# Loading the next batch's x in four pieces, and projecting inside the third group of heads

## What is computed

```python
q = split_heads(x @ Wq.T + bq)              # x: (8, 1024, 512)
k = split_heads(x @ Wk.T + bk)
v = split_heads(x @ Wv.T + bv)
q_lr = jnp.einsum('bhtd,hdr->bhtr', q, Wq_lsr)
k_lr = jnp.einsum('bhtd,hdr->bhtr', k, Wk_lsr)
scores = jnp.einsum('bhir,bhjr->bhij', q_lr, k_lr) * scale
scores = jnp.where(causal_mask, jnp.float32(-jnp.inf), scores)
y = jnp.einsum('bhij,bhjd->bhid', _softmax(scores), v)
x = _layernorm(x + y.transpose(0, 2, 1, 3).reshape(Bq, Tq, D_MODEL) @ Wo.T + bo)
```

## Time and profile before

| | us |
|---|---|
| median of 3 runs | 3893.7 (3890.47 to 3897.09) |
| the profiled execution, in all | 3893.05 |
| its span on the core | 3891.3 |
| TensorE busy | 3630.7 (93%) |
| VectorE busy | 2260.8 (58%) |
| ScalarE busy | 1488.4 (38%) |
| GpSimd busy | 666.7 (17%) |

### The profile page before, as it was taken

One profiled execution on the slowest core, in us unless ns is written; L12 is line 12 of the kernel. 1 busy time (PEld: TensorE's weight loads), 2 busy tenths in 40 slices (PEclk: granted clock), 3 DMA queues, 4 the chain that ended last, 5 costly groups with the idle time before them and its releaser, 6 DMA issues. The chain is left out here.

```text
span 3891.3 us, 55460 instructions
## 1 busy us (share of the span) xinstructions
PE 3630.7 (93%) x19935; PEld 2505.5 (64%) x19935; DVE 2260.8 (58%) x4972; ACT 1488.4 (38%) x2793; POOL 666.7 (17%) x859
## 2 busy tenths in 40 slices
PE   4899999999999999999999737999999999999995
PEld 3555556556555555565555337888888888888884
DVE  2576665675765766657657475444444444544456
ACT  1253443443444434434434322333333333333335
POOL 2022121121121221211211201011111111111113
PEclk8999999999999999999999855999999999999997
DMA  5234234233323252332332203343343343444448
GB/s 169 61 93 127 76 92 123 62 97 112 102 72 113 79 142 64 101 110 71 89 115 66 72 0 99 100 139 117 112 131 111 120 124 111 130 121 117 143 157 308
DMA packets 207200, 423.14 MB, mean 109 GB/s; under 512 B 45840, under 2 KB 48912, under 8 KB 198800
## 3 DMA queue, kind: packets, MB, share of 16 engines
q1 hardware_dynamic: 180304, 367.47, 30.6%
q0 software_dynamic: 14400, 35.14, 4.6%
q10 hardware_dynamic: 12288, 17.83, 1.7%
HBM read 246.23 MB, written 72.38 MB: 82 GB/s over the span
## 5 line engine op out<-in xcount | busy, mean ns | idle before, releaser
L833 ACT ACTIVATE probs<-scores_t 128x512 f32<-128x512 f32 (+3 forms) x1536 | 656.8, 496 | 574.6 <-PE scores_t L700 516.9
L1801 PE MATMUL m_ps_h<-m_tokens_t,m_w_parts 128*128 128x512 f32 x3072 | 739.7, 391 | 1.6 <-DVE m_tokens_t L1683 1.6
L1801 PE MATMUL m_ps_y<-m_w_parts,m_hidden_parts 128*128 128x512 f32 x3072 | 737.3, 390 | 0.6
L1801 PEld LDWEIGHTS m_ps_y<-m_w_parts,m_hidden_parts 128*128 128x128 f32 x3072 | 575.3, 188 | 125.8 <-issue 6.3
L1801 PEld LDWEIGHTS m_ps_h<-m_tokens_t,m_w_parts 128*128 128x128 f32 x3072 | 575.3, 188 | 120.1 <-issue 2.0
L889 DVE CUSTOM_DVE_ANT_0 shared_banks<-shared_banks,mask_q_rows 128x128 f32<-128x128 f32 (+3 forms) x1024 | 477.7, 515 | 176.4 <-PE shared_banks L657 173.9
L657 PE MATMUL shared_banks<-k_operands,q_operands 96*128 96x512 f32 (+3 forms) x1536 | 509.3, 379 | 23.7 <-DVE natural L880 8.9
L700 PE MATMUL scores_t<-q_operands,k_operands 128*128 128x512 f32 (+3 forms) x1536 | 494.7, 372 | 33.3 <-ACT probs L833 26.1
L1619 ACT ACTIVATE m_hidden<-m_ps_h,m_b 128x512 f32<-128x512 f32 x256 | 176.6, 690 | 791.1 <-PE m_ps_h L1801 777.9
L562 POOL TENSOR_SCALAR_AFFINE_SELECT probs<-probs 128x256 f32<-128x256 f32 x512 | 220.3, 433 | 1341.3 <-ACT probs L833 1340.7
L657 PEld LDWEIGHTS shared_banks<-k_operands,q_operands 96*128 96x128 f32 x1536 | 279.0, 191 | 263.7 <-issue 122.9
(11 more groups left out here) (243 smaller groups left out, 3225.2 us busy)
## 6 DMA issues: line engine op xcount, KB each, us to landing
m_w_raw<-in_w1T SPq DMA_DIRECT2D x64, 1024.0 KB, 5.2
m_w_raw<-in_w2T SPq DMA_DIRECT2D x64, 1024.0 KB, 7.5
wqk_group<-scratch_wqk SPq DMA_DIRECT2D x32, 1024.0 KB, 5.6
q_operands<-natural SPq DMA_DIRECT2D x192, 128.0 KB, 2.6
k_operands<-natural SPq DMA_DIRECT2D x192, 128.0 KB, 2.7
q_operands<-natural SPq DMA_DIRECT2D x384, 64.0 KB, 2.0
k_operands<-natural SPq DMA_DIRECT2D x384, 64.0 KB, 2.0
natural<-in_xT SPq DMA_DIRECT2D x8, 2048.0 KB, 9.8
```

Source lines behind the costliest of these rows:

```text
L833: act.activation(probs[:, slot_of(k, h // 2), h % 2, c0:HALF], st[:, (HG * k + h) % SCORE_BANKS, c0:HALF], ACT.Exp, scale=SCALE).then_inc( ...
L1801: mm = pe.matmul(bank, a, b, start=(first and n == 0), stop=(final and n == len(pairs) - 1))
```

## The change

1. The next batch's x is loaded in four DMAs of 32 partitions (512 KB each). The piece of head h - 1 is issued behind the strips of head h in slot 1's end, and waits only for the strips of head h - 1; the last piece waits for head 3's. The weights that were issued ahead of x now follow it. The first x of the program is also four DMAs.
2. Slot 2 projects its lower halves at positions 38 and 43 instead of 46 and 47, and copies the lower strips inside the slot (`HALVED` = 3); at its end only upper strips remain.
3. ScalarE's copies of x move from (7, 0), (7, 2), (8, 0), (8, 2) to (5, 2), (6, 0), (6, 2), (7, 0); GpSimd's subtraction from weigh 6 to weigh 3; VectorE's from (8, 3) to (7, 1).
4. Slot 3 uses the same table and order of maxima, and the same inversions, as the slots before it. It had a table of its own, by whole heads, whose first maximum came at position 9.

```diff
-HALVED = 2
+HALVED = 3
-MAX_EARLY = (1, 1, 0, 2, 0, 2, 2, 1, 0, 0, 2, 1, 0, 0, 0, 3, 0, 0, 1, 1,
...
-MAX_LATE = (0, 0, 0, 0, 0, 0, 0, 0, 0, 2, 2, 1, 1, 0, 3, 0, 0, 0, 3, 0,
...
-MAX_AFTER = (MAX_EARLY,) * 3 + (MAX_LATE,)
-PROJ_AFTER = ((27, 42, 56, 57),) * HALVED + ((46, 47, 56, 57),) * 2
+MAX_AFTER = (1, 1, 0, 2, 0, 2, 2, 1, 0, 0, 2, 1, 0, 0, 0, 3, 0, 0, 1, 1,
...
+PROJ_AFTER = ((27, 42, 56, 57),) * 2 + ((38, 43, 56, 57), (46, 47, 56, 57))
-X_HI_AT = ((7, 0), (7, 2), (8, 0), (8, 2))
+X_HI_AT = ((5, 2), (6, 0), (6, 2), (7, 0))
-X_LO_AT = 6
-X_LO_DVE_AT = (8, 3)
-INVERT_AFTER = ((((30, 36, 42, 45), (2, 6, 10, 14)),) * 3 + (((30, 42, 45, 45), (0, 4, 4, 5)),))
+X_LO_AT = 3
+X_LO_DVE_AT = (7, 1)
+INVERT_AFTER = ((30, 36, 42, 45), (2, 6, 10, 14))
...
-            def load_x(b, n):
-
-                for h in range(HG):
-                    sp.wait_ge(strips_sent[h], n * STRIPS)
-                for half in lower_sent:
-                    sp.wait_ge(half, n // GROUPS * HALVED * LOWER_STRIPS)
-                sp.dma_start(nat[:], xT_dram.rearrange("(c p) t -> p c t", p=P)[:, :, bass.ds(b * T, T)]
+            def load_x(b, h):
+
+                rows = slice(DH * h, DH * h + DH)
+                sp.wait_ge(strips_sent[h], b * GROUPS * STRIPS)
+                sp.wait_ge(lower_sent[h // 2], (b * HALVED - 1) * LOWER_STRIPS)
+                sp.dma_start(nat[rows], xT_dram.rearrange("(c p) t -> p c t", p=P)[rows, :, bass.ds(b * T, T)]
                              ).then_inc(x_in, 16)
...
+                    if x_of is not None and h > 0:
+                        load_x(x_of, h - 1)
+                if x_of is not None:
+                    load_x(x_of, HG - 1)
...
+                lower_strips(b, 0)
+                strips(b, 0, first=HALF, weights=GROUPS - 1)
+                lower_strips(b, 1)
+                strips(b, 1, first=HALF, x_of=b + 1 if more else None)
                 if more:
-                    load_x(b + 1, b * GROUPS + GROUPS)
-                    strips(b, GROUPS - 2)
+                    load_w(0)
+                    lower_strips(b, 2)
+                    strips(b, 2, first=HALF)
                     load_w(1)
...
-                                act.wait_ge(x_in, 16 * (b + 2))
+                                act.wait_ge(x_in, 16 * HG * (b + 2))
```

More of the change, by code:

```diff
@@ L237, in plan_slot @@
         order += [("proj", g, i) for i, at in enumerate(PROJ_AFTER[g]) if at == n]
[L238 removed]
+        order += [("invert", g, 0, i) for i, at in enumerate(INVERT_AFTER[0]) if at == n]
         if g > 0:
[L240 to L242 removed]
+            order += [("invert", g - 1, 1, i) for i, at in enumerate(INVERT_AFTER[1]) if at == n]
+        order += [("max", g, i) for i in range(done, done + MAX_AFTER[n])]
+        done += MAX_AFTER[n]
         if n == JOIN_AFTER:
@@ L356, in build_attention @@
         LOWER_STRIPS = STRIPS * HG // 2
-        steps, maxes = attend_steps(), [max_steps(g) for g in range(GROUPS)]
+        steps, halves_first, by_head = attend_steps(), max_steps(False), max_steps(True)
         NE = len(steps)
@@ L455, in lower_strips, with strips @@
                                          ).then_inc(lower_sent[h // 2], 16)
-            def strips(b, slot, lead=False, heads=range(HG), first=0, weights=None):
+            def strips(b, slot, lead=False, heads=range(HG), first=0, weights=None, x_of=None):
                 g = (slot + AHEAD) % GROUPS
@@ L474, in strips @@
                                      ).then_inc(strips_sent[h], 16)
+                    if x_of is not None and h > 0:
+                        load_x(x_of, h - 1)
+                if x_of is not None:
+                    load_x(x_of, HG - 1)
             def run(b):
                 more = not (b == NB - 1)
-                for slot in range(HALVED):
-                    lower_strips(b, slot)
-                    early = slot + 1 < HALVED
-                    strips(b, slot, first=HALF, weights=(slot + AHEAD + 1) % GROUPS if early else None)
-                    if more and not early:
-                        load_w((slot + AHEAD + 1) % GROUPS)
+                lower_strips(b, 0)
+                strips(b, 0, first=HALF, weights=GROUPS - 1)
+                lower_strips(b, 1)
+                strips(b, 1, first=HALF, x_of=b + 1 if more else None)
                 if more:
-                    load_x(b + 1, b * GROUPS + GROUPS)
-                    strips(b, GROUPS - 2)
+                    load_w(0)
+                    lower_strips(b, 2)
+                    strips(b, 2, first=HALF)
                     load_w(1)
@@ L511, in store @@
                 sp.dma_start(table[bass.ds(b * T + t * P, P), 0:D], xn[:, t % 2]).then_inc(xn_out[t % 2], 16)
-            load_x(0, 0)
+            for h in range(HG):
+                rows = slice(DH * h, DH * h + DH)
+                sp.dma_start(nat[rows], xT_dram.rearrange("(c p) t -> p c t", p=P)[rows, :, 0:T]).then_inc(x_in, 16)
             load_w(0)
@@ L884, in run @@
                     elif kind == "max":
-                        h, slot, it, k0, n = maxes[item[1]][item[2]]
+                        h, slot, it, k0, n = (by_head if lead else halves_first)[item[2]]
                         dve.wait_ge(bank_full[bank], off[bank] + turn + 1)
```

10 lines of the change are left out of this document (4 added, 6 removed).

## The result

| | before | after |
|---|---|---|
| median, us | 3893.7 | 3953.6 (3952.2 to 3955.4) |
| ratio, 95% interval | 1 | 1.0154 (1.0136 to 1.0172) |
| span of the profiled execution, us | 3891.3 | 3953.7 |
| slot 2, sum over seven batches | 392.2 | 461.1 |
| slot 3, batch 3 | 52.1 | 50.2 |

The change makes the kernel slower by 60 us, 1.5%. The forecast was 3930 us with a range from 3895 to 3962; sign and range held, and the loss was 1.6 times the one forecast.

What follows compares the result with a forecast made beforehand. TensorE, busy 93% of the span, was taken as the bound, losing time in slot 2 to late x and lower clock. Slot 2 +49.2, slot 3 -14 and start +1.5 gave +36.7 us: 3930 us, range 3895 to 3962.

Steps and rivals of the forecast that it cites:

- Term A: Slot 2: ScalarE asks for x before it lands, so TensorE waits 5.0 us before a score of step 6.
- lower clock behind A: Slot 2: after the gap at step 6's score TensorE runs at its lower clock, losing 2.9 us.
- Term B: Slot 2: VectorE's moved subtractions precede a maximum that frees a bank, so TensorE waits 2.85 us near step 7.
- lower clock behind B: Slot 2: TensorE's second gap, waiting for VectorE, brings a second stretch of lower clock, losing 2.0 us.
- banks behind the projections: Slot 2: the second maximum behind the projection waits 0.3 us for the bank VectorE frees after the projection's copy.
- The rival on slow pieces: Load of x: 32-row pieces take 6.2 us to land, making TensorE's gap 6.9 us; 3944 us, chance 0.18.
- Term C: Slot 3: its maxima can begin at once, giving slot 0's length: 2.1 us less per batch, 14 us in seven.
- The start: Program start: first x in four pieces means three more issues ahead of its landing, taken as 1.5 us more.
- rival 1: Slot 2: x's pieces land in time, so the wait for x and its clock loss vanish; 3875 us, chance 0.09.
- rival 2: Slot 2: VectorE's subtractions are covered, only the place of the wait moves; no change, 3894 us, chance 0.15.
- rival 4: Slot 3: lower strips late or another bound, so the 14 us gain is missing; 3944 us, chance 0.10.

Runs made afterwards that it cites:

- e3_places_only: Kernel before with only the change's slot 2 places for copies, subtractions and projections; x in one DMA behind the weights, slot 3 as before: 3974.9 us.
- e2_pieces_only: Kernel before with only the change's load of the next x: four pieces of 32 rows between the strips, weights behind; old places: 3876.0 us.
- e5_one_dma: Changed kernel with every x, the first too, in one DMA on 128 partitions instead of four row pieces: 3940.8 us.
- e4_gpsimd_splits: Changed kernel with all four subtractions for x on GpSimd and none on VectorE: 3941.4 us.
- e8: Changed kernel, x in four column pieces with own semaphores, the engines' old places for x, slot 2's lower projections at 43 and 46: 3853.4 us.
- e7: Kernel before, x in four column pieces ahead of the weights, a semaphore for each, old places: 3852.3 us.
- e6_column_pieces: Changed kernel, x in four column pieces on 128 partitions, a semaphore for each, the change's places kept: 3916.4 us.
- e1_swap: Kernel before with the next x, still one DMA, issued ahead of the weights instead of behind them: 3874.2 us.

## Why the prediction was right, and where its sizes were off

Per batch, above 50.0 us in slot 2:

| term | predicted | measured |
|---|---|---|
| A: gap before the score of step 6 | 5.0 (3.8 to 6.9) | 8.1 in batch 3, 7.7 to 9.0 in all |
| lower clock behind A | 2.9 | 2.75 |
| B: VectorE before the maximum | 2.85 | 2.15 |
| lower clock behind B | 2.0 | 0 (1.6 in batch 0) |
| banks behind the projections | 0.3 | 1.6 |
| without a gap | 0 | 0.9 |
| sum | 13.05 | 15.5 (batch 3), 15.9 (mean) |

*The mechanism was right.* All the places at which the forecast saw TensorE stand are in the trace, each with the releaser named, and e3_places_only and e2_pieces_only give the signs that the forecast gave to the two halves: places +80 us, load -18 us. One of its signs failed: the second stretch of lower clock, seen in one slot of seven. That the total was off by only 24 us is in part luck, since errors of up to some 3 us a batch stood on both sides: A, the banks and what shows in no gap were forecast too small by 5.3 us together, B and the clock too large by 2.85.

*Term A was sized too small, beyond its upper bound.* Two steps failed. "1059.3 + 2.26 = 1061.6" took the wait for head 3's strips over from a queue without pieces. With pieces in the queue the wait was 3.2 to 4.2 us in the seven batches; with none, in e5_one_dma, it was 2.1 to 2.2 us in six of them. (The second piece lies ahead of these strips and the third beside them; which of the two holds them up was not tried.) The fourth piece went out 20.5 us into the slot, not 18.5. And "I take 4.3 us" for the landing was 5.5: between 3.1 and 6.2 I leaned to the line of the 128-partition rows, although the strips on 32 partitions were the nearer rows. Together x came 26.0 us into the slot instead of 22.8. The rival on slow pieces had the second of these causes, and with 3944 us it is nearer to the measured time than the forecast.

*The clock was sized too large*: 4.9 us against 2.75, or 2.9 on the mean of the seven slots. The first term, 2.9 us behind A, was right in size, but by luck: the gap was 8.1 us and not 5.0, and the lower clock began inside it, so that 4.7 us of the stretch at 1.2 GHz were free. The step that failed is the second term: "A second gap brings a second stretch of lower clock" was so in batch 0 alone, and its 2.0 us were 0.2 on the mean. e4_gpsimd_splits took the second gap away and left the clock of batch 2's slot at 0.92.

*Term B* was 0.7 us too large: in its new place VectorE's pair took 2.40 us, not 2.98. The 2.98 us were read where GpSimd was still subtracting: it ended at 1072.96 + 4.70 = 1077.66, after VectorE had begun at 1077.11, and VectorE's first subtraction ended 1.08 us after that. In the changed kernel GpSimd had ended 2 us before VectorE began, and each subtraction took 1.22 us. The remaining 0.1 us was not followed up. *The banks behind the projections* were 1.6 us instead of 0.3: I counted one of the two places, and for it only a part of the copy through ScalarE and VectorE.

*Term C* was right: 50.2 us, 13 us of the 14, and e8 against e7 shows it again. *The start* cost 4.7 us instead of 1.5, inside its bounds; with one DMA (e5) it was 0.3 us: the half rate again.

*The other rivals.* x did not come in time (rival 1). VectorE's pair wasn't covered (rival 2), with e4_gpsimd_splits as its measure. Slot 3 did what the change says (rival 4).

## What to carry to other kernels

An engine that runs its list in order pays for a place twice: if it comes before its data, everything behind it waits; and having its data earlier doesn't help a step if the list ahead of it isn't done. So compare the time at which the data lands with the time at which the place is reached, for each engine that touches them, before a table is changed. Cut a load along the dimension that keeps all partitions, give each piece its semaphore, and put it ahead of transfers that are needed later: here that alone was worth 41 us (1%), of which the order alone gave 20. The changed tables gained 13 us in slot 3 and, at their best places, gave that back in slot 2. Columns and semaphores were always changed together, so what each is worth alone is not shown.

## What the runs showed of the hardware that was not expected

- Pieces of 32 partitions moved 199 to 212 GB/s at a DMA share of 0.99 to 1.05 (233 in one window of 2 us), one DMA on 128 partitions 395 to 432 GB/s at the same share. The busy share of the DMA engines doesn't tell these apart.
- The lower clock behind a gap doesn't grow with the gap as far as the work is concerned. In slot 2 of the kernel before, gaps of 3.4 to 3.8 us cost 3.2 to 3.4 us of clock; in that of the changed kernel, gaps of 7.7 to 9.0 us cost 2.4 to 3.1 us behind them, since part of the time at 1.2 GHz lay inside the gap.
- A second gap of 2.0 to 2.2 us, some 7 us behind the end of a long one, was followed by another stretch at 1.2 GHz in 9 of the 28 slots 2 that had it (one of seven in the changed kernel, four in e3_places_only, two each in e5_one_dma and e6_column_pieces). Gaps of 0.44, 0.75 and 0.74 us spread over 7 us in e1_swap left the clock at its higher level.
- A running GpSimd instruction holds up VectorE's subtraction. In all kernels here, a subtraction that began beside an idle GpSimd took 1.22 us, and one that began with 0.3 us or more of a GpSimd instruction still to run ended 1.07 to 1.09 us after that instruction, so that it took 1.42 to 2.17 us.
- Copies that were never late still left slot 2 at 50.6 us, 0.6 above slot 0; where they were late by 1.5 to 3.2 us (e1_swap), slot 2 took about 1 us more than its gaps explain. The cause of this 1 us stays open.
